# The output matrix of the attention is split in SBUF and turned by transposing DMAs

## The reference

```
tok_h  = token stage (an S4D filter bank) of x        # [64 batches, 128 tokens, 1024]
for each of the 64 batches, h = tok_h[b]:
  n    = layernorm(h)
  q, k, v = n wq^T, n wk^T, n wv^T                    # 32 query heads, 8 kv heads, head size 32
  q, k = rope(q), rope(k)
  att  = softmax(mask(q k^T / sqrt(32))) v
  y    = h + att wo^T                                 # wo is the output matrix, 1024 x 1024
  out  = y + ffn(layernorm(y))                        # W_base, four LoRA experts, a router
```

## Time and profile before

| | before |
| --- | --- |
| median of three runs | 2895.41 us |
| profiled execution, own time | 2895.14 us |
| its span in the trace | 2893.2 us |
| TensorE busy | 2799.6 us (97%) |
| from 345 to 2800 us | TensorE busy 2455.0 of 2455 us |
| granted clock, mean | 0.991 |

### The profile page before, as it was taken

The page is one execution under the profiler, slowest core; times in us unless marked ns, Lnnn a source line. Parts: engine busy times, 40 slices in busy tenths (PEclk is TensorE's granted clock), DMA queues, the critical chain, the costliest instruction groups (busy, mean ns, idle before and its releaser), DMA issues.

```text
span 2893.2 us, 61884 instructions
## 1 busy us (share of the span) xinstructions
PE 2799.6 (97%) x16932; PEld 1408.5 (49%) x16932; DVE 2366.2 (82%) x8776; ACT 1918.2 (66%) x5986; POOL 1970.2 (68%) x1730
## 2 busy tenths in 40 slices
PE   6788899999999999999999999999999999999997
PEld 5665444444444444444444444444444444444443
DVE  9987788888888888888888888888888888888784
ACT  8887766666666666666666666666666666666662
POOL 4542677777777776777777777777767777777763
PEclk9999899999999999999999999999999999999999
DMA  7884677666666666666666666666666666666763
GB/s 246 231 217 135 142 153 150 149 149 151 151 143 152 146 156 147 151 149 147 152 148 149 149 150 151 143 152 147 156 149 148 150 146 152 150 149 149 152 132 78
DMA packets 1220851, 442.64 MB, mean 153 GB/s; under 512 B 1167120, under 2 KB 1175568, under 8 KB 1220640
## 3 DMA queue, kind: packets, MB, share of 16 engines
q1 hardware_dynamic: 1220640, 440.69, 66.7%
HBM read 88.22 MB, written 67.11 MB: 54 GB/s over the span
## 4 chain that ended last, share of the span: by engine, by line
PE 89%; DVE 3%; DMA 3%; ACT 2%; issue 1%; POOL 1%; SPq 1%; DVEq 0%; ACTq 0%; POOLq 0%
PE bank_b L2068 44%; PE bank_a L2068 22%; PE bank_c L2068 11%; PE score L2031 4%; PE kps L581 2%; PE pv L2057 2%; DMA tok_h<-kout 2%; PE bank_b L2057 1%; PE bank_b L2227 1%; DMA xc<-in_x_dram 1%; PE pv L2160 1%; ACT kout L358 1%; ACT probs L1440 0%; PE bank_c L2121 0%; PE pv L2121 0%
## 5 line engine op out<-in xcount | busy, mean ns | idle before, releaser
L1440 ACT ACTIVATE probs<-probs,negmax 128x128 f32<-128x128 f32 x2016 | 777.3, 387 | 247.4 <-DVE negmax L1658 247.3
L1303 POOL TENSOR_TENSOR p_hl<-probs,p_hl 128x512 f16<-128x512 f32 x503 | 607.6, 1208 | 333.9 <-ACT p_hl L1449 331.4
L1299 POOL TENSOR_TENSOR probs<-probs,rsum 128x512 f32<-128x512 f32 x503 | 547.6, 1089 | 183.5 <-DVE rsum L1669 183.1
L1658 DVE CUSTOM_DVE_ANT_0 probs<-score,table,scal 128x128 f32<-128x128 f32 x2016 | 589.0, 347 | 78.1 <-issue 77.4
L2068 PE MATMUL bank_a<-qkv_hi,xt 128*128 128x512 f16 x2048 | 642.6, 380 | 2.0 <-DMA xt<-xy_hl 2.0
L2068 PE MATMUL bank_b<-b_hi,yt 128*128 128x512 f16 x1952 | 610.7, 379 | 0.0
L1449 ACT ACTIVATE p_hl<-probs 128x512 f16<-128x512 f32 x503 | 314.5, 625 | 417.8 <-POOL probs L1299 417.8
L1712 DVE TENSOR_TENSOR heads<-rope_a,heads 128x512 f16<-128x512 f32 x319 | 388.1, 1232 | 30.0 <-ACT heads L1470 29.9
L2068 PE MATMUL bank_a<-qkv_lo,xt 128*128 128x512 f16 x1024 | 389.7, 381 | 0.0
L1440 ACT ACTIVATION_READ_ACCUMULATOR probs<-probs,negmax 128x1 f32 x2016 | 376.5, 187 | 0.0
L2068 PE MATMUL bank_b<-o_hi,at_hi 128*128 128x512 f16 x992 | 376.4, 379 | 0.0
(11 more groups left out here) (311 smaller groups left out, 4590.2 us busy)
## 6 DMA issues: line engine op xcount, KB each, us to landing
hin<-tok_h SPq DMA_DIRECT2D x64, 512.0 KB, 3.2
r<-tok_h SPq DMA_DIRECT2D x64, 512.0 KB, 3.8
out_dram<-r SPq DMA_DIRECT2D x63, 512.0 KB, 3.0
tok_h<-kout SPq DMA_DIRECT2D x60, 512.0 KB, 6.1
probs_t<-p_hl SPq DMA_TRANSPOSE x512, 3.1
xc<-in_x_dram SPq DMA_DIRECT2D x32, 128.0 KB, 4.5
raw_a<-in_L_attn_wq_dram SPq DMA_DIRECT2D x4, 1024.0 KB, 9.2
raw_b<-in_L_attn_wo_dram SPq DMA_DIRECT2D x8, 512.0 KB, 4.8
```

What stands on the lines that cost most here:

```text
L1299: TT(x, x, rsum[:, u % 4].unsqueeze(2).to_broadcast([P, GR, T]), ALU.mult).then_inc(s_norm, 1)
L1303: TT(p_hl[:, u % 2, 1], probs[:, u % 4], p_hl[:, u % 2, 0], ALU.subtract).then_inc(s_plo, 1)
L1440: ins = A(probs[:, u % 4, g], probs[:, u % 4, g], ACT.Exp, bias=negmax[:, u % 4, g:g + 1], scale=-1.0, accum_out=sums[:, u % 4, g:g + 1])
L1658: ins = V.tensor_tensor_reduce(probs[:, u % 4, g], score[u % 2][:, g], mask, col(U_SC), 3e38, ALU.add, ALU.min, negmax[:, u % 4, g:g + 1])
```

## The change

wo is no longer among TensorE's jobs. Each block i of 128 rows is split as it lies in SBUF, in three steps, and then two DMA transposes, one for each half, write it turned into `o_hi` and `o_lo` (`o_turn`). The new order of columns is made by the split: it reads 32-element pieces in one order and writes them in the other (`from_order`, `to_order`).

Who does the steps depends on the block. Blocks 0 and 1: POOL makes the high half (two instructions of 128x512), scales the raw block in place (one of 128x1024), makes the low half (two of 128x512). Blocks 2 and 3: POOL scales, ACT makes the high half (two of 128x512), POOL the low half. Blocks 4 to 7: ACT makes the high half (two, with the scale), DVE the low half in eight instructions of 128x128 (`o_low`). The halves of block i lie where the raw block i-1 was, so block i's high half waits until the low half of block i-1 is done; block 0 uses the bias's tile, and block 4 the first two parts of `heads`.

Beside that: `kv(0)` now waits until all 24 qkv jobs are done; `spread(4)` moves from ahead of `kv(0)` to behind its third chunk; `pe_close` is gone; `base_sums` is spread as two, two and four, the last four ahead of batch 1's norm instead of two behind it; the bias is loaded after block 0 is turned; the first query heads wait for block 4, ACT's first `b_hi` and the first use of wo for all blocks.

```diff
-            jobs.append((raw_b[:, i], i, a, "o"))
+        def halves_of(i):
+            row_ = spare[i // HALF] if i % HALF == 0 else raw_b[:, i - 1].bitcast(F16)
+            return row_[:, 0:D], row_[:, D:2 * D]
+        def to_order(x, a):
+            return x[:, a * 512:(a + 1) * 512].rearrange("p (c k d) -> p c k d", c=GR, k=4)
+        def from_order(i, a):
+            return raw_b[:, i, a * 512:(a + 1) * 512].rearrange("p (k c d) -> p c k d", c=GR, k=4)
+        def o_turn(sp, i):
+            sp.wait_ge(s_olp, i + 1)            # for i >= 4: s_olv, i - HALF + 1
+            for part, name in zip(halves_of(i), ("o_hi", "o_lo")):
+                sp.dma_start_transpose(keep[name][:, :, i * P:(i + 1) * P], part).then_inc(s_ot[i], 16)
...
+        def act_after(act):                     # o_high: two Copy of 128x512
+            Prep.high(act, 14, J_B)
+            Prep.o_high(act, HALF)
+            Prep.o_high(act, 2)
+            Prep.o_high(act, 3)
+            Prep.o_high(act, HALF + 1)
             act.wait_ge(s_scal[3], 1)           # and lbs behind it
...
-                base_sums(0, 4)
+                base_sums(0, 2); Prep.o_high(act, HALF + 2)     # turn -1, k = 0
-                base_sums(4, 6)
+                base_sums(2, 4); Prep.o_high(act, HALF + 3)     # k = 2
+                base_sums(4, NO)                                # k = 3
-                Prep.high(act, MID, MID + 4); base_sums(6, NO)  # "norm"
-                Prep.high(act, MID + 4, J_B)                    # "last"
...
+            def o_low(i):                       # DVE
+                for a in range(2):
+                    for k in range(4):
+                        ins = STT(lo[:, :, k], raw[:, :, k], col(S_O), hi[:, :, k], ALU.mult, ALU.subtract)
-                low(J_O, MID)
+                o_low(HALF)                     # after(), ahead of lbs
+                if b == -1 and k == "start": o_low(HALF + 1)
+                if b == -1 and k == 0: o_low(HALF + 2)
+                if b == -1 and k == "v": o_low(HALF + 3)
...
-            Prep.turn(pe, 10, MID)
-            Prep.spread(pe, 4)
+            Prep.turn(pe, 10, J_B)
-                    prep.pe_close(pe)
+            prep.o_high_pool(pool, 0); prep.o_scale(pool, 0); prep.o_low_pool(pool, 0)
             at(turn, -2)
+            prep.o_high_pool(pool, 1); prep.o_scale(pool, 1); prep.o_low_pool(pool, 1)
+            prep.o_scale(pool, 2); prep.o_scale(pool, 3); prep.o_low_pool(pool, 2); prep.o_low_pool(pool, 3)
             turns(pool, turn)
```

More of the change, by code:

```diff
@@ L719, in high @@
                     act.wait_ge(w["s_v"], NCH)
+                if j == J_B:
+                    for done in s_ot:
+                        act.wait_ge(done, 32)
                 act.wait_ge(s_wt, j + 1)
@@ L762, in act_early @@
             if b == -1 and k == 0:
[L763 removed]
+                base_sums(0, 2)
+                Prep.o_high(act, HALF + 2)
             if b == -1 and k == 2:
[L765 to L771 removed]
+                base_sums(2, 4)
+                Prep.o_high(act, HALF + 3)
+            if b == -1 and k == 3:
+                base_sums(4, NO)
+            if b == 0 and isinstance(k, int):
                 Prep.high(act, J_B + 2 * k, J_B + 2 * k + 2)
@@ L874, in early @@
             def early(b, k):
+                if b == -1 and k == "start":
+                    o_low(HALF + 1)
+                if b == -1 and k == 0:
+                    o_low(HALF + 2)
+                if b == -1 and k == "v":
+                    o_low(HALF + 3)
                 if b == -1 and k == "last":
-                    low(MID, MID + 4)
                     dve.wait_ge(s_sums, NO)
@@ L914, in turn @@
                     pe.wait_ge(s_wlo, before[j])
[L915 to L924, removed]
+                for c in range(4):
+                    ins = nc.tensor.transpose(place(j)[:, c], raw[:, (4 * a + c) * P:(4 * a + c + 1) * P], idt)
                 ins.then_inc(s_wt, 1)
@@ L1196, in turn @@
                     turn_heads(n, "k")
+                if qkv and not attention:
+                    prep.o_turn(sp, NO - 2)
+                    prep.o_turn(sp, NO - 1)
                 if attention:
@@ L1282, in _ @@
             prep.bias_load(sp)
+            prep.o_turn(sp, 1)
+            for i in range(2):
+                prep.o_turn(sp, NO // 2 + i)
+                prep.o_turn(sp, 2 + i)
             for b in range(-1, CB - 1):
@@ L2103, in wo @@
                         pe.wait_ge(s_alo, p * 2 + 2)
+                        if not some(p):
+                            for done in prep.o_in:
+                                pe.wait_ge(done, 32)
                     if c0 == 0 and finish:
@@ L2126, in turn @@
                     scores(0)
-                if qkv:
+                if qkv and not attention:
+                    pe.wait_ge(prep.wlo, prep.jb)
+                    kv(0, 3)
+                    prep.spread(pe, 4)
+                    kv(3, 7)
+                elif qkv:
                     kv(0, 7)
```

110 lines of the change are left out of this document (87 added, 23 removed).

## The result

| | before | after |
| --- | --- | --- |
| median of 7 runs each | 2895.05 us | 2905.00 us |
| lowest to highest | 2892.99 to 2898.27 | 2902.29 to 2907.47 |
| ratio, 95% interval | | 1.0036 [1.0026, 1.0045] |
| profiled execution, its span | 2895.14, 2893.2 us | 2905.14, 2903.3 us |
| TensorE busy, mean granted clock | 2799.6 us, 0.991 | 2790.0 us, 0.988 |

The changed kernel is 9.95 us (0.34%) slower: on the side that the prediction held for likelier, inside its range, 4 us past its number. TensorE is busy for 9.6 us less, and the whole takes longer by about as much.

A forecast was written before the change was run, and what follows sets the result against it. The prediction took batch 1's norm chain, which releases `kv` through `xt`, as the new bound: +4.1 us, plus 1.6 for the clock, gives +5.7 on 2895.1, about 2901 us; range 2893.5 to 2911.

The forecast's parts named there:

- What ends last: Ahead of batch 1's `kv`: with the turns gone from TensorE, the norm's chain to `xt` becomes the bound.
- The rival in which the removed turns and the added waits cancel: Norm late within its 4.4 us slack, or the hole at 283 us absorbs it: 2894 to 2897 us; chance 0.16.
- `kv(0)` 4.5 us earlier: On TensorE, `kv(0)` starts near 231.1 instead of 235.58 us; the gain is idle time.
- `lbs` 3.6 us late through ACT's waits for POOL: On ACT, waits for POOL's scalings and halves of blocks 1 to 3 delay `lbs` by 3.6 us.
- the strided rival: On POOL, access in 32-element pieces makes a half take 1.68 us (2904) or 3.2 us (2913); chance 0.12.
- the faster rival: POOL's halves take about 0.6 us, ACT never waits, batch 1's `kv` starts 8.9 us earlier: 2886 us; chance 0.07.
- `o_low` at 1.7 us a block: On DVE, eight 128x128 low-half instructions at 0.21 us each; with the late `lbs`, statistics 7.5 us late.
- Four base sums ahead of `xy_hl`: On ACT, four sums at 1.24 us each end at 259.5, starting `xy_hl` 1.1 us later than the norm allows.
- Landing at 268.2, +4.1: Batch 1's `xt` lands at 268.2 us, against `kv`'s former start at 264.12: +4.1 us.
- The clock, +1.6: TensorE, idle ahead of batch 1's `kv`, then runs at a lower clock: +1.6 us, bounds 0 and 2.8.
- SP's queue hidden, cover 3.6 us: On SP, 14 more transposes clear by 260.5 us, before `xt` is ready at 264.1: no cost.
- The sum: Whole kernel: +4.1 us for the norm's chain and +1.6 for the clock, together +5.7 us, about 2901 us.

The follow-up runs named there:

- norm_first: Kernel after, with block 7's two halves, its transposes and the last four `base_sums` moved behind batch 1's norm; 2902.79 us, ratio to before 1.0029.
- the second profile: The kernel after, unedited, profiled once more; 2902.22 us.
- warm: Kernel after, with 72 unused 128x512 matmuls on TensorE behind `q(1)` and 12 behind the first two b jobs; 2899.83 us, ratio to before 1.0024.
- scale_early: Kernel after, with POOL scaling blocks 2 and 3 ahead of block 0; 2906.02 us, ratio to before 1.0051.
- joint: Kernel after, with one 512 KB transpose per block instead of two of 256 KB; 2904.01 us, ratio to before 1.0037.
- reordered: Kernel after, with joint transposes, early scalings, `lbs` ahead of block 5 on ACT and later pieces behind batch 1's norm; 2895.62 us, ratio to before 1.0004.
- reordered_warm: The reordered kernel with 44 unused matmuls added behind `q(1)`; 2893.93 us, ratio to before 1.0000.
- low4_out: Kernel after, with DVE writing zeros instead of block 4's low half; 2901.97 us, ratio to before 1.0035.

## Why the prediction was right, and where it fell short

- *What ends last.* Right. TensorE is idle for the 14.80 us ahead of 264.45, `kv` of batch 1 is released by `xt`, and `xt` by the norm. The rival in which the removed turns and the added waits cancel is out: the hole behind `kv` of batch 1 gave nothing back (`scores(1)` 7.66 us late, `kv` of batch 2 7.66). `scores(0)`, which was to be no later, is 0.6 us later from r0 (264.45 and 262.75).
- *`kv(0)` 4.5 us earlier.* 232.03 against 235.58 is 3.6, and 4.7 counted from r0. Idle time, as said.
- *`lbs` 3.6 us late through ACT's waits for POOL.* Measured 3.0 from r0. POOL's high halves took 1.04 us (L743) and its low halves 1.16 (L753), the medians of L1299 and L1303 in the earlier trace rows: the 32-element pieces cost POOL nothing that shows. So the strided rival is out, though the measured time alone lies nearer to its 2904 than to 2901, and a half of 0.6 us, which the faster rival needed, does not occur.
- *`o_low` at 1.7 us a block.* Mis-sized: 2.19, 2.19 and 2.62. Eight in 2.19 us are 0.27 us each, above my upper bound of 0.24, and `lbs` 0.6 us sooner than forecast hides a part of it. With the late `lbs` the statistics are 8.2 us late from r0, where I had 7.5.
- *Four base sums ahead of `xy_hl`.* Right: `xy_hl` starts 39.6 us after r0, 30.6 before, 9.0 later (forecast 259.5 - 250.94 = 8.6). norm_first puts the price of these sums and block 7 at 3.6 us of the chain.
- *Landing at 268.2, +4.1.* `kv` starts 4.8 us later, from r0; the other 1.1 of the 5.95 is the shift between the two profiles.
- *The clock, +1.6.* 6.24 - 4.53 = 1.7, in the second profile 2.4; warm confirms it. The upper bound of 2.8 was too low: the step of 5.64 us from 264.12 to 269.76 in the kernel before ran at full clock, and at half it would take 5.6 more.
- *SP's queue hidden, cover 3.6 us.* The result was right, the cover too large: 1.5 us. Behind the first two, a transpose took 1.31 to 1.37 us, under the point of 1.56, but those two sat 9.1 us in the queue, which the sum had not, nor the load of `hin` (0.58 us). Scaling early uses this cover up.
- *The sum.* Through `kv` of batch 2 it is 6.5 us from r0 (89.6 - 83.1), close to the 5.7. What failed is the sentence that from 345 us on the work would only move as a whole: between `kv` of batch 2 and the scores that start at 482.96 us (470.98 before) the kernel after loses 4.3 us more (11.98 - 7.66, against the first profile of before; 3.15 in its second profile), some 2 us of it at the two gaps of PE at 381 and 403 us above, and gains back 1.9 by the end. No term stood for that.

Why these steps lose stays open. Counted in the same way, the loss is 3.4 us in norm_first, 3.2 in scale_early, 2.5 in joint, 1.55 in warm, 0.75 in reordered and 3.4 in reordered_warm, which reaches `kv` of batch 2 2.5 us earlier than before, from r0. low4_out arrives within 0.6 us of the kernel after and loses nothing (-0.2), so arriving late does not by itself bring the loss. DVE's busy time from 500 to 2800 us goes a part of the way with it: 1890.3 us in the kernel before, 1888.5 in low4_out, 1916.1 in the kernel after; but warm has 1912.9, and reordered_warm 1900.7. These are one profile a kernel, two for before and after. That a batch's `xt` sets a floor there whatever TensorE brings along is argued from the waits for `xt`, not shown.

## What to carry to other kernels

Taking work off the busiest engine pays only where that engine is what ends last: here the turns filled a time in which the next batch's norm was being made, and the same time became idle and at half clock. Follow the moved pieces on each engine to the first instruction behind them that somebody waits for, and put that one first; after that look at the queue behind it, which was 1.5 us away from being the bound. A change that opens a gap in front of TensorE can also pay for the clock in the step behind it, here 1.7 to 2.4 us.

## What the runs showed of the hardware

In these rows DVE waits for POOL, one whole instruction at a time. Block 4's eight subtractions on DVE, 128x128 with two SBUF inputs, stand beside POOL's scalings and halves. Here are the first, the third and the fifth of them, with the POOL instruction beside each of the first two:

```profile
233.24 1.93 POOL L731 TENSOR_TENSOR raw_b<-raw_b,scal 128x1024 f32<-128x1024 f32 x1
233.35 1.98 DVE L944 SCALAR_TENSOR_TENSOR heads<-raw_b,scal,heads 128x128 f16<-128x128 f32 x1
...
237.04 1.20 POOL L753 TENSOR_TENSOR raw_b<-raw_b 128x512 f16<-128x512 f32 x1
237.15 1.24 DVE L944 SCALAR_TENSOR_TENSOR heads<-raw_b,scal,heads 128x128 f16<-128x128 f32 x1
...
239.47 0.34 DVE L944 SCALAR_TENSOR_TENSOR heads<-raw_b,scal,heads 128x128 f16<-128x128 f32 x1
```

POOL works without a break from 233.24 to 239.40 and then waits until 240.78 (its timeline above). While it works, DVE finishes one instruction for each of POOL's four, each 0.15 us behind the end of POOL's: two of 1.98 us beside the scalings, two of 1.24 beside the halves. As soon as POOL stops, the other four take 0.34 us each. So the price follows the length of POOL's instruction. In the second profile of the kernel after the same group met one scaling and two halves and took 5.63 us, and in scale_early two halves alone and took 3.98.

Two stretches of 1 us, with DVE's busy time of these eight, the count of instructions touched, PEclk, DMA share and GB/s, show that the DMAs are not what slows them, since their share is the same with POOL at work and without:

```profile
237.20:238.20 1.00, 1.00 (x2) 1.00 1.01 414
239.20:240.20 1.00, 1.00 (x4) 1.00 1.00 406
```

Over the span, the lines of both engines (ns min/median/max):

```profile
L944 DVE SCALAR_TENSOR_TENSOR raw_b<-raw_b,scal x24: 340/347/783, 245.9 to 256.8; 128x128 f16<-128x128 f32 x24
```

```profile
L753 POOL TENSOR_TENSOR raw_b<-raw_b x6: 1155/1156/1200, 231.0 to 241.9; 128x512 f16<-128x512 f32 x6
```

POOL paid little: 1.20 us for a half beside DVE, 1.16 otherwise (1.35 once, in scale_early). DVE's low halves of wq, wk and wv, which read one input from PSUM and one from SBUF, were not slowed beside POOL: ten took 6.68 us from 225.30 on, with POOL at work from 226.86, and 6.92 before, with POOL idle from 225.8. The prediction weighed the contention the other way round, as up to 2.9 us on POOL. It cost next to nothing here (low4_out), since DVE had the time.

The Trainium skill ("GPSIMD Engine Reference", section 1 Specifications) has the two engines share their SBUF interfaces, with contention under VectorE instructions of two SBUF inputs. The trace agrees: such an instruction took up to 1.98 us instead of 0.34.

A second thing is the queue. The first transpose of 256 KB that SP issues behind the loads of W_base sat 6.02 us in its queue, where the median of that line is 1.33; joint's first of 512 KB sat 9.38 us.
